# Small matmuls on zeros in TensorE's order: 74 groups in the first sequence of a Mamba and mixture-of-experts layer

## The reference

```python
xz = layernorm(x) @ W_in + b_in             # 128 -> 512
u, z = split(xz); u = silu(u)               # 256 each
B, C = split(u @ W_xproj + b_xproj)         # 16 states each
dt = softplus(u @ W_dt + b_dt)
h = h * exp(dt * A) + dt * u * B            # step by step over 512 tokens
y = sum over states of h * C + D * u
x = x + (y * silu(z)) @ W_out + b_out
scores = softmax(layernorm(x) @ gate_w.T)   # 8 experts, the best 2 by score + bias
x = x + sum_e weight_e * mlp_e(layernorm(x)) + mlp_shared(layernorm(x))
```

## Time and profile before

| | value |
|---|---|
| time, median of 3 runs | 1208.53 us (1208.41 to 1209.28) |
| the profiled execution: time, span | 1208.65 us, 1206.8 us |
| mean granted TensorE clock | 0.975 |
| PE busy, share of the span | 1125.5 us, 93% |
| PE weight loads (PEld) | 949.5 us, 79% |
| DVE busy | 1092.8 us, 91% |
| ACT busy | 1091.0 us, 90% |
| POOL busy | 1048.5 us, 87% |
| instructions | 21930 |

### The profile page before, as it was taken

The page is one execution under the profiler, slowest core; times in us unless marked ns, Lnnn a source line. Parts: engine busy times, 40 slices in busy tenths (PEclk is TensorE's granted clock), DMA queues, the critical chain, the costliest instruction groups (busy, mean ns, idle before and its releaser), DMA issues.

```text
span 1206.8 us, 21930 instructions
## 1 busy us (share of the span) xinstructions
PE 1125.5 (93%) x7352; PEld 949.5 (79%) x7352; DVE 1092.8 (91%) x1666; ACT 1091.0 (90%) x1916; POOL 1048.5 (87%) x459
## 2 busy tenths in 40 slices
PE   6467788899999999999999999999999999999998
PEld 4345677788888888888878888888888888788887
DVE  4898999999999999999999999999999999899744
ACT  5668989999999999999999999999999999999763
POOL 3899989999999999999999999999999998788400
PEclk7778999999999999999999999999999999999999
DMA  7552333416060522507052340706143150430000
GB/s 239 223 209 82 142 157 117 183 38 262 19 282 24 203 100 82 219 18 281 27 212 88 127 182 12 288 18 250 50 163 146 64 236 10 182 118 1 19 9 10
DMA packets 49456, 153.68 MB, mean 127 GB/s; under 512 B 4416, under 2 KB 31424, under 8 KB 32832
## 3 DMA queue, kind: packets, MB, share of 16 engines
q1 hardware_dynamic: 49344, 152.28, 32.6%
HBM read 147.03 MB, written 5.24 MB: 126 GB/s over the span
## 4 chain that ended last, share of the span: by engine, by line
POOL 45%; PE 27%; issue 15%; ACT 6%; DVE 4%; DMA 1%; SPq 1%; POOLq 0%; DVEq 0%; ACTq 0%
POOL dbu L785 23%; POOL hc L795 18%; PE h L989 12%; PE mixed L996 8%; PE y_acc L1079 4%; DVE hc L902 2%; ACT da L689 2%; POOL res L764 1%; POOL w_s L772 1%; ACT L689 1%; DMA below<-in_below 1%; POOL rstd L756 1%; DVE g L951 1%; PE mixed L989 1%; ACT silu L723 1%
## 5 line engine op out<-in xcount | busy, mean ns | idle before, releaser
L785 POOL TENSOR_TENSOR dbu<-w_s,b_all 128x2048 f32<-128x2048 f32 x128 | 585.8, 4577 | 19.9 <-DMA b_all<-bc_rows 19.9
L795 POOL TENSOR_TENSOR hc<-hc,c_all 128x1024 f32<-128x1024 f32 x151 | 359.2, 2382 | 51.7 <-DVE hc L902 51.2
L689 ACT ACTIVATE da<-dt_s,a_neg 128x512 f32<-128x512 f32 x512 | 346.0, 691 | 46.6 <-DVE hc L902 24.1
L902 DVE TENSOR_TENSOR_SCAN hc<-da,dbu 128x512 f32<-128x512 f32 x302 | 358.5, 1211 | 22.8 <-PE y_acc L1079 11.6
L1079 PE MATMUL y_acc<-ident,hc 128*128 128x128 f32 x2048 | 297.6, 282 | 43.3 <-POOL hc L795 30.7
L1079 PEld LDWEIGHTS y_acc<-ident,hc 128*128 128x128 f32 x2048 | 248.8, 145 | 97.8 <-POOL hc L795 41.1
L996 PEld LDWEIGHTS mixed<-w_s,g 128*128 128x128 f32 x2304 | 273.4, 193 | 26.0 <-DVE g L951 13.2
L996 PE MATMUL mixed<-w_s,g 128*128 128x128 f32 x2304 | 285.2, 277 | 8.9 <-DVE g L951 6.3
L902 DVE TENSOR_TENSOR_SCAN da<-da,dbu 128x512 f32<-128x512 f32 x210 | 252.7, 1218 | 16.0 <-POOL dbu L785 10.3
L989 PE MATMUL h<-x_hi,w_hi 128*128 128x512 f32 x576 | 257.5, 447 | 5.8 <-DVE g L951 4.3
L989 PE MATMUL h<-x_lo,w_hi 128*128 128x512 f32 x576 | 227.9, 396 | 0.0
(11 more groups left out here) (84 smaller groups left out, 922.7 us busy)
## 6 DMA issues: line engine op xcount, KB each, us to landing
b_all<-bc_rows SPq DMA_DIRECT2D x64, 1024.0 KB, 6.4
c_all<-bc_rows SPq DMA_DIRECT2D x64, 1024.0 KB, 8.8
xt<-in_x SPq DMA_DIRECT2D x16, 256.0 KB, 2.9
res<-in_x SPq DMA_DIRECT2D x16, 256.0 KB, 3.0
out<-acc SPq DMA_DIRECT2D x16, 256.0 KB, 2.3
silu<-in_w SPq DMA_DIRECT2D x6, 256.0 KB, 4.5
w_s<-in_w SPq DMA_DIRECT2D x1, 1152.0 KB, 12.0
bc_rows<-bc_rows_s SPq DMA_DIRECT2D x16, 64.0 KB
```

The source lines that it names most:

```text
L689: act.activation(da[a % DA_SLOTS][:, :], dt_s[:, m % DT_SLOTS, c, :], ACT.Exp, scale=a_neg[:, a:a + 1]).then_inc(decay_made, 1)
L785: pool.tensor_tensor(dbu[:, at:at + AT_ONCE, :], w_s[:, c, None, :].broadcast_to([P, AT_ONCE, T]), b_all[:, s:s + AT_ONCE, :], ALU.mult).t ...
L795: pool.tensor_tensor(pair, pair, c_all[:, s:s + 2, :], ALU.mult).then_inc(c_by_pool, 1)
L902: dve.tensor_tensor_scan(dst, ring[:, :], dbu[:, a % DBU_SLOTS, :], 0.0, ALU.mult, ALU.add).then_inc(scanned, 1)
```

## The change

74 entries `warm.0` are put in PE's order of the start, between z.0 of sequence 0 and red.6 of sequence 1. Each is one group of four matmuls on zeros. All other entries of PE, and the orders of the other engines, are as before. With the number of groups in parentheses, they stand: z.0 (6) z.1 (7) dl.1 (1) red.0 (2) red.1 (2) red.2 (2) red.3, x_t.0+1 (1) red.4 (2) red.5 (7) red.6 to red.9 (4) xp.0+1, xp.1+1 (1) red.10 to red.13 (7) red.14 to red.17 (2) red.18 to red.20 (1) gy.0, red.21 (6) red.22 to red.25 (8) red.26 to red.29 (2) red.30, red.31 (1) gy.1 (2) red.0+1, proj.0, z.0+1, red.1+1, z.1+1 (1) red.2+1, red.3+1 (1) red.4+1, red.5+1, x_t.0+2 (8) red.6+1.

```diff
 START_ORDER = {
     "pe": """
-        x_t.0 xp.0 xp.1 bc.0 dl.0 z.0 z.1 dl.1 red.0 red.1 red.2 red.3 x_t.0+1 red.4 red.5 red.6 red.7 red.8
-        red.9 xp.0+1 xp.1+1 red.10 bc.0+1 red.11 red.12 red.13 red.14 red.15 dl.0+1 dl.1+1 red.16 red.17
...
+        x_t.0 xp.0 xp.1 bc.0 dl.0 z.0 warm.0 warm.0 warm.0 warm.0 warm.0 warm.0 z.1 warm.0 warm.0 warm.0
+        warm.0 warm.0 warm.0 warm.0 dl.1 warm.0 red.0 warm.0 warm.0 red.1 warm.0 warm.0 red.2 warm.0 warm.0
+        red.3 x_t.0+1 warm.0 red.4 warm.0 warm.0 red.5 warm.0 warm.0 warm.0 warm.0 warm.0 warm.0 warm.0
...
+        z.1+1 warm.0 red.2+1 red.3+1 warm.0 red.4+1 red.5+1 x_t.0+2 warm.0 warm.0 warm.0 warm.0 warm.0
+        warm.0 warm.0 warm.0 red.6+1 split.0 red.7+1 red.8+1 red.9+1 xp.0+2 xp.1+2 h1.0 h1.1 h3.0 red.10+1
```

The rest of the diff brings code for three options that are off: TURNED_FIRST and HI_BY_DVE are empty lists and PAIRED is 0, so their tasks (bt, wt, td, tb, padd) are in no order, and the counts that replace the old ones come out the same. It also allocates two unused buffers (b_turned, w_turned) and three unused semaphores, and ACT's `whi` tasks now wait for their DMA each time instead of once in three:

```diff
                 if what == "whi":
-                    if a % RAW == 0:
-                        act.wait_ge(raw_in[a // RAW], 16 * RAW)
+                    act.wait_ge(raw_in[a // RAW], 16 * RAW)
```

More of the change, by code:

```diff
@@ L52, with turned, dbu_count, turned_count @@
 ]
+TURNED_FIRST = []
+def turned(m):
+    return TURNED_FIRST[m] if m < len(TURNED_FIRST) else []
+def dbu_count(step, m):
+    own = [g for g in range(step // AT_ONCE + 1) if g not in turned(m)]
+    return sum(DBUS - len(turned(k)) for k in range(m)) + len(own)
+def turned_count(step, m):
+    own = [a for a in range(step + 1) if a // AT_ONCE in turned(m)]
+    return AT_ONCE * sum(len(turned(k)) for k in range(m)) + len(own)
+PAIRED = 0
+def in_pairs(m):
+    return m >= SEQS - PAIRED
+def sums(m):
+    return range(0, STEPS, 2) if in_pairs(m) else range(STEPS)
+def sum_count(step, m):
+    return sum(len(sums(k)) for k in range(m)) + len([a for a in sums(m) if a <= step])
+def pair_count(step, m):
+    return STEPS // 2 * (m - (SEQS - PAIRED)) + step // 2 + 1
 def by_dve(m):
@@ L111 @@
[L111 to L115, removed]
@@ L291 @@
 START_TO, END_FROM = 3, SEQS - 1 - 1
-MIXED = ("x_t", "xp", "z", "bc", "dl", "gy", "proj", "split", "route", "eo")
+MIXED = ("x_t", "xp", "z", "bc", "dl", "gy", "proj", "split", "route", "eo", "bt", "wt", "td")
 UNIT = ("h1", "h3")
@@ L308, in __init__ @@
         self.place = {task: i for i, task in enumerate(self.order)}
+        self.signals, self.before = [0] * banks, {}
+        for i, task in enumerate(self.order):
+            self.before[task] = self.signals[i % banks]
+            self.signals[i % banks] += task[0] != "td"
     def bank(self, name, a, m):
-        use = self.place[name, a, m]
-        return use % self.banks, use // self.banks
+        return self.place[name, a, m] % self.banks, self.before[name, a, m]
     def user_before(self, name, a, m):
@@ L503, in c_count, with hc_free @@
             return c_by_pool, sum(len(by_pool(k)) // 2 for k in range(m)) + by_pool(m).index(a) // 2 + 1
+        def hc_free(a, m):
+            user, back = before(a, HC_SLOTS, STEPS)
+            if m < back:
+                return reduced, 0
+            if in_pairs(m - back) and user % 2:
+                return pair_added, pair_count(user, m - back)
+            return reduced, sum_count(user, m - back)
         def mixed_tile(name, a, m):
@@ L521, in taken, with wait_bank @@
             return mixed_freed[which], uses + 1
+        def wait_bank(eng, name, a, m):
+            which, signals = bank_of(name, a, m)
+            user = MIXED_TURN.user_before(name, a, m)
+            if user and user[0] == "td":
+                eng.wait_ge(scanned, STEPS * user[2] + user[1] + 1)
+            else:
+                wait(eng, mixed_freed[which], signals)
         def windows(name, task):
@@ L668, in task @@
                                    bias=bdt_s[:, a:a + 1]).then_inc(freed, 1)
+                elif what == "btc":
+                    wait(act, turned_made, turned_count(-1, m))
+                    act.activation(b_turned[:, :], tile[:, 0:P], ACT.Copy).then_inc(freed, 1)
+                elif what == "wtc":
+                    wait(act, turned_made, turned_count(NS * a - 1, m))
+                    act.activation(w_turned[:, :], tile[:, :], ACT.Copy).then_inc(freed, 1)
+                elif what == "tb":
+                    c, s = a // NS, a % NS
+                    act.wait_ge(*taken("bt", 0, m))
+                    act.wait_ge(*taken("wt", c, m))
+                    user, back = before(a, DBU_SLOTS, STEPS)
+                    if not (first and back):
+                        act.wait_ge(scanned, STEPS * (m - back) + user + 1)
+                    for b in range(NB):
+                        last = act.activation(as_blocks(dbu[:, a % DBU_SLOTS, :])[:, b, :], as_blocks(w_turned)[:, b, :],
+                                              ACT.Copy, scale=b_turned[:, 2 * NS * b + s:2 * NS * b + s + 1])
+                    last.then_inc(turned_made, 1)
                 elif what == "skip":
                     act.wait_ge(*taken("xp", a, m))
-                    which, uses = bank_of("gy", a, m)
-                    wait(act, mixed_freed[which], uses)
-                    act.activation(mixed[which][:, :], u[:, m % U_SLOTS, a, :], ACT.Copy,
+                    wait_bank(act, "gy", a, m)
+                    act.activation(mixed_tile("gy", a, m)[:, :], u[:, m % U_SLOTS, a, :], ACT.Copy,
                                    scale=d_s[:, a:a + 1]).then_inc(skip_made, 1)
@@ L681, in task @@
                             act.wait_ge(const_steps, 2)
[L683 to L690, removed]
+                    if a // AT_ONCE in turned(m):
+                        act.wait_ge(mixed_written, use_of("td", a, m))
+                        dst = dbu[:, a % DBU_SLOTS, :]
+                    else:
+                        dst = da[a % DA_SLOTS][:, :]
+                        user, back = before(a, DA_SLOTS, STEPS)
+                        if not (first and back):
+                            if user in by_dve(m - back):
+                                act.wait_ge(*c_count(user, m - back))
+                            else:
+                                act.wait_ge(scanned, STEPS * (m - back) + user + 1)
+                    act.activation(dst, dt_s[:, m % DT_SLOTS, c, :], ACT.Exp, scale=a_neg[:, a:a + 1]).then_inc(decay_made, 1)
                 elif what == "ycopy":
-                    act.wait_ge(reduced, STEPS * m + NS * (a + 1))
+                    act.wait_ge(reduced, sum_count(NS * (a + 1) - 1, m))
                     if a == 1:
@@ L1029, in task @@
                         pe.wait_ge(g_made, UNITS * m + NF * (a + 1))
-                    which, uses = bank_of(what, a, m)
-                    tile = mixed[which]
+                    tile = mixed_tile(what, a, m)
                     if what != "gy":
-                        wait(pe, mixed_freed[which], uses)
-                    if what == "x_t":
+                        wait_bank(pe, what, a, m)
+                    if what == "bt":
+                        last = pe.matmul(tile[:, 0:P], bc_rows[:, :], ident[:, :], is_transpose=True, start=True, stop=True)
+                    elif what == "wt":
+                        last = transposes(tile, as_blocks(w_s[:, a, :]))
+                    elif what == "td":
+                        last = transposes(tile, as_blocks(dbu[:, a % DBU_SLOTS, :]))
+                    elif what == "x_t":
                         last = transposes(tile, xt)
```

89 lines of the change are left out of this document (64 added, 25 removed).

## The result

The changed kernel takes 1206.98 us, the median of 17 runs (1205.42 to 1208.76); beside it the kernel before took 1209.95 (1206.96 to 1212.33). The ratio is 0.9977, with a 95% interval of 0.9970 to 0.9984: 2.8 us faster (1.9 to 3.6). The forecast was 1.0 us faster, 1207.5 us. The range held, the direction was right, the size was a third.

What follows compares the result with a forecast made beforehand. POOL was taken to set the pace until 112 us, the chain passing through PE at 106.5. Faster reds there give -1.3 us, 0.3 lost: -1.0 us from the 1208.53 median, 1207.5 us; range 1204.5 to 1211.5.

Steps and rivals of the forecast that it cites:

- Price and fit: PE's stretch of 88.8 us: 74 groups at 0.68 us are 50.3 us, existing work 30 us, so 80 us fit.
- Lost at the landing of b_all: Whatever PE wins before 48 us is lost, since POOL starts dbu.3 at 48.34 when that DMA lands.
- projc.0 and the lead of DVE: proj.0 starts at 93.04 as now, ends 1.7 us sooner; DVE's 1.41 us wait goes, not yet time won.
- the place without margin: Before red.6+1: the last 8 groups, 5.4 us, end at 106.5, its gate; without DVE's lead at 108.1.
- Red.6+1, split.0, red.7+1: On the chain from 106.5 us: 2.84 us at half clock become 1.5 us, scan.11+1 up to 1.3 us sooner.
- -1.3 us at 109, of which I let 0.3 be lost: The gain at scan.11+1, less 0.3 us for tables and orders on ACT and POOL: -1.0 us.
- later falls change too: Rival, 17%: a shift spares PE's half-clock falls at 124 to 128 and 168 to 174 us; near 1204.5 us.
- likeliest case: -1.0 us, cashed between 106 and 136 us, own range 1206.6 to 1208.3; 46%.
- The range and the chances: 1204.5 to 1211.5 us; with 2.4 us as what can be told: faster 16%, same 65%, slower 19%.
- The slower rival: 19%: PE becomes late where the clock falls inside the stretch, groups costing 1.25 us; +4 us, about 1212.5.

Runs made afterwards that it cites:

- e2: Changed kernel with only the early 34 groups, ahead of xp.1 of sequence 1; ratio to the kernel before 0.9996 (0.9986 to 1.0006).
- e4: Changed kernel with only the last 8 groups, ahead of red.6+1; ratio to the kernel before 1.0001 (0.9993 to 1.001).
- e10: Changed kernel without the last 8 groups ahead of red.6+1, 66 groups left; ratio to the kernel before 0.9989 (0.9980 to 0.9997).
- e3: Changed kernel with only the late 40 groups, from xp.1 of sequence 1 on; ratio to the kernel before 0.9985 (0.9976 to 0.9994).
- e7: Changed kernel with 4 more groups in the first 14 us; ratio to the kernel before 0.9977 (0.9968 to 0.9986).
- e8: Changed kernel with 5 more groups ahead of red.6+2 and 3 ahead of red.18+2; ratio to the kernel before 1.0001 (0.9991 to 1.0011).
- e9: The changed kernel measured again, unaltered; ratio to the kernel before 0.9980 (0.9971 to 0.9989).
- e12: Changed kernel with the 74 groups on softplus weights instead of zeros; ratio to the kernel before 0.9979 (0.9970 to 0.9988).
- e11: Changed kernel with none of the 74 groups, but 4 added in the first 14 us; ratio to the kernel before 1.0000 (0.9991 to 1.001).
- e1: Changed kernel with all 74 groups taken out, rest of the diff kept; ratio to the kernel before 1.0001 (0.9992 to 1.001).
- e6: Changed kernel with 16 groups instead of the last 8 ahead of red.6+1; ratio to the kernel before 1.0023, median 1211.97 us.

## Why the prediction was right, and where its size was off

- **Price and fit: right.** 0.68 us per group was predicted and 0.68 us (8 x 0.085) measured; PE is busy 84.69 of 88.80 us where I had 80 in total by start-to-start times. Dl.1 ended at 30.5 us instead of 29.6, since z.0 ended a microsecond later in this launch, with half clock until 18 us; that cost nothing, as POOL's next product waits for the DMA.
- **Lost at the landing of b_all: right.** e2 gains nothing measurable, and dbu.3 moves with the first dbu in the trace of the changed kernel (-0.45 and -0.39).
- **projc.0 and the lead of DVE: right.** The 1.41 us are gone, x_t.0+2 ends at 100.7, and the last eight groups end on their gate. e4 and e10 show that this is the place without margin, as I had it: without the last eight the gain is 0.65 us, with them alone there is a loss of 0.50.
- **Red.6+1, split.0, red.7+1: right.** Scan.11+1 starts 1.05 us sooner relative to POOL (1.5 sooner, of which 0.45 is this launch's start); I had up to 1.3.
- **The step that was mis-sized: "-1.3 us at 109, of which I let 0.3 be lost".** Scan.11+1 brings 1.05 us, of which 0.66 are left ahead of scan.18+1, since DVE waits for POOL's dbu.4+1 in between. The wait of scan.18+1 for PE brings another 1.11, so that hcp.18+1 gains 1.77 us (1.74 to 1.78 in e3, e7, e8, e9 and e12, which also run at full clock at 106 us). I had this wait in the rival "later falls change too" and set against it that "the idle time ahead of them is unchanged". That was wrong for the fall at 124 us: the lead shortens PE's wait before route.0 from 1.49 to 0.44 us. In all six traces with 0.44 there is no fall from 112 to 140 us; of the eight with 1.49 to 1.94 us seven have one there, and e11 has none. For the fall near 170 it was right: PE idles 2.98 us there before and 3.57 after, and the fall stays. So likeliest case and rival were one case in part. (The rival's sum is off too: 1208.5 - 1.0 - 3.5 is 1204.0, not 1204.5.)
- **Left out: what is given back.** Resb.0+1 waits for the DMA of res. SP issues it 2.21 us sooner (146.01 instead of 148.22), but it lands only about 1.5 us sooner; POOL waits 2.06 instead of 1.36 us. That returns 0.75 us in the changed kernel and 0.8 in e9 and e12, but nothing in e7. By hcp.6+2 the trace of the changed kernel keeps 1.23 us over dbu.4+1, e7's 1.82, those of e9 and e12, whose clock also falls at 149 to 155 us, 0.2. At the end of the span the changed kernel's trace is 1.3 us ahead, 0.45 of which it had at the first dbu. So the pair of traces that I forecast gives 0.9 us, close to my 1.0, but by a larger gain and a loss that I had not seen: in part luck.
- **Launches: most of the missing size, and open.** The traces show less than the 2.8 us over many launches. First, both are single launches: the trace of before, at 1208.65 us, is on the cheap side (39 of all 116 launches of that kernel are as fast or faster), that of the changed kernel, at 1207.29, is 0.3 us above the median of its 17. Second, my sum took the falls of one trace as those of the kernel. From the first dbu to the end of the span, the traces of before, e1 and e11 differ by 0, +0.6 and +3.5 us, and those of the changed kernel, e9, e12 and e7 by -0.9, +0.1, +0.2 and -1.8 us. The means are 2.0 us apart, but these are three and four launches that scatter as widely. Without groups a fall can cost where the trace of before lost nothing (1.43 us at 74 us in e11); with all 74 there is no fall between 20 and 112 us in any of five traces. But 2.4 of e11's 3.5 us are lost behind hcp.6+2, past all groups, and no run shows whether the groups have a part in that. How often such falls occur is not counted, so 1 to 2 of the 2.8 us have no shown cause beyond e1, which says that they come with the groups.
- **The range and the chances.** In absolute time 1206.98 lies inside the likeliest case's own 1206.6 to 1208.3, but that is luck: the kernel before measured 1209.95 beside it and not 1208.53. As a difference, 2.8 us is beyond that case's 0.2 to 1.9 and between it and the rival. I gave 16% to a gain of over 2.4 us, which is what came.
- **The slower rival** was priced rightly in its kind: e6 turns it on, at 5.0 to 5.6 us for eight groups too many. In the change itself the clock never fell inside the stretch.

No kernel here beats the changed one: e7's 1206.73 us and e9's 1206.56 cannot be told apart.

## What to carry to other kernels

Filling an engine's idle time to hold its clock pays only where that engine ends a wait on the chain; here that is proj.0, whose lead carries on to red.6+1, and red.6+1 with what follows; the other groups keep the clock up until then. A lead can also shorten an idle gap further on and take away the fall behind it, as before route.0, so recompute later gaps before calling them unchanged. Fill a gap up to its gate and not past it: groups too many cost about their full length, as does one that has to wait for a bank. When a clock falls at different places in each launch, one trace of before is one draw; subtract the start times of the bounding engine's instructions trace from trace before reading a difference of a microsecond.

## What the runs showed of the hardware that was not expected

- The fall of the clock in the first 18 us comes in some launches and not in others of the same order: five of the twelve traces without extra groups at the start had it, and POOL's first product starts 0.7 to 2.3 us later in these than in the others.
- Behind PE's wait before route.0 the clock falls in seven of the eight traces where that wait is 1.49 to 1.94 us, and in none of the six where it is 0.44 us.
- In the opening groups of the trace of before the records give a clock of 1.00, while the instructions run at half speed for the first 3 us or so the earlier trace rows; durations have to be read there.
- A DMA of 256 KB (res) that is issued 2.21 us sooner among the same 1 MB transfers landed 1.5 us sooner: 10.8 instead of 10.1 us from issue to its user's start.
